# Who issues the last two transfers of score maxima in a fused two-layer cross-attention kernel

## The reference, cut to what matters

```python
q = hidden_state @ Wq + bq
k = encoder_hidden_state @ Wk + bk
v = encoder_hidden_state @ Wv + bv
scores = jnp.einsum('bkgld,bksd->bkgls', q, k) * scale + mask
attn = jax.nn.softmax(scores, axis=-1)
out = jnp.einsum('bkgls,bksd->bkgld', attn, v)
# ... output projection, residual, layer norm
```

## Time and profile before

| what | value |
|---|---|
| median of 3 runs | 886.73 us (885.75 to 888.23) |
| the profiled execution | 885.36 us, span 883.5 us |
| PE busy | 786.0 us, 89% |
| DVE busy | 597.9 us, 68% |
| ACT busy | 488.3 us, 55% |
| POOL busy | 561.7 us, 64% |
| mean granted TensorE clock | 0.943 of full speed |
| issues of qstack<-mrep | 64 by SPq, 128 KB each |

### The profile page before, as it was taken

The page is one execution under the profiler, slowest core; times in us unless marked ns, Lnnn a source line. Parts: engine busy times, 40 slices in busy tenths (PEclk is TensorE's granted clock), DMA queues, the critical chain, the costliest instruction groups (busy, mean ns, idle before and its releaser), DMA issues.

```text
span 883.5 us, 17327 instructions
## 1 busy us (share of the span) xinstructions
PE 786.0 (89%) x5015; PEld 619.9 (70%) x5015; DVE 597.9 (68%) x1016; ACT 488.3 (55%) x1067; POOL 561.7 (64%) x769
## 2 busy tenths in 40 slices
PE   6699989899898989989898999989899998988662
PEld 5576868678586867868686786868778686866431
DVE  4785948768485785858577685858768585866633
ACT  5547474655737465573746557374655747465050
POOL 3937494865858577585857658494866749473144
PEclk9989999999999999999999999999999999999776
DMA  8233252514334251433525143352514325242420
GB/s 315 65 102 96 73 132 90 144 56 112 101 101 119 86 144 66 110 104 101 125 86 150 58 115 96 100 131 89 142 62 118 99 89 131 89 96 72 101 84 24
DMA packets 58764, 92.23 MB, mean 104 GB/s; under 512 B 10480, under 2 KB 28528, under 8 KB 58608
## 3 DMA queue, kind: packets, MB, share of 16 engines
q1 hardware_dynamic: 58016, 91.60, 36.8%
q10 hardware_dynamic: 720, 0.28, 0.2%
HBM read 24.72 MB, written 8.39 MB: 37 GB/s over the span
## 4 chain that ended last, share of the span: by engine, by line
PE 62%; SPq 13%; DVE 8%; DMA 6%; issue 5%; POOL 5%; ACT 1%; DVEq 0%; POOLq 0%; ACTq 0%
PE banks L781 13%; SPq L373 12%; PE banks L872 11%; PE banks L885 7%; DMA qstack<-mrep 4%; PE banks L897 4%; DVE maxima L1527 4%; PE banks L899 4%; PE banks L898 4%; PE banks L819 3%; POOL atl L618 3%; PE banks L821 3%; PE banks L820 3%; PE banks L843 2%; DVE ql L1520 2%
## 5 line engine op out<-in xcount | busy, mean ns | idle before, releaser
L1477 DVE TENSOR_REDUCE negmax<-banks 128x1 f32<-128x512 f32 x128 | 84.5, 682 | 139.1 <-PE banks L768 139.1
L1527 DVE TENSOR_REDUCE maxima<-banks 128x4 f32<-128x512 f32 x256 | 160.1, 683 | 12.6 <-PE banks L843 12.5
L1184 ACT ACTIVATE prob<-banks 128x512 f32<-128x512 f32 x256 | 133.8, 607 | 33.8 <-PE banks L872 32.5
L872 PE MATMUL banks<-qstack,kstack 128*128 128x512 f32 x256 | 101.4, 527 | 39.4 <-DMA qstack<-mrep 38.9
L781 PEld LDWEIGHTS banks<-ta,att 128*128 128x128 f32 x1024 | 119.0, 190 | 4.1 <-POOL ta L553 1.3
L781 PE MATMUL banks<-ta,att 128*128 128x130 f32 x1024 | 119.6, 275 | 0.9 <-POOL ta L553 0.9
L872 PEld LDWEIGHTS banks<-qstack,kstack 128*128 128x128 f32 x256 | 61.1, 247 | 84.3 <-issue 74.2
L1553 DVE RECIPROCAL dens<-dens 128x512 f32<-128x512 f32 x32 | 107.1, 3346 | 17.3 <-DMA dens<-sides 17.3
L1118 ACT ACTIVATE att<-banks,negmax 128x512 f32<-128x512 f32 x128 | 87.4, 685 | 47.4 <-DVE negmax L1477 47.4
L618 POOL TENSOR_TENSOR atl<-at,ath 128x512 fp32r<-128x512 f32 x32 | 47.0, 1468 | 99.5 <-ACT ath L1196 99.5
L1169 ACT ACTIVATE qh<-banks,bq_s 128x256 fp32r<-128x256 f32 x64 | 30.4, 476 | 92.2 <-PE banks L821 92.2
(11 more groups left out here) (144 smaller groups left out, 1950.4 us busy)
## 6 DMA issues: line engine op xcount, KB each, us to landing
qstack<-qh SPq DMA_DIRECT2D x128, 128.0 KB, 2.3
xs<-in_x SPq DMA_DIRECT2D x16, 512.0 KB, 3.7
ys<-in_ctx SPq DMA_DIRECT2D x16, 512.0 KB, 3.7
kstack<-kph SPq DMA_DIRECT2D x128, 64.0 KB, 2.0
qstack<-ql SPq DMA_DIRECT2D x64, 128.0 KB, 2.3
qstack<-mrep SPq DMA_DIRECT2D x64, 128.0 KB, 2.3
dens<-sides SPq DMA_DIRECT2D x64, 128.0 KB, 2.0
out_x<-late SPq DMA_DIRECT2D x32, 256.0 KB, 2.1
```

What stands on the lines that cost most here:

```text
L872: last = mm(o, kstack[:, j, 2 * p + odd], qstack[:, p, j], start=True, stop=not masked)
L1184: nc.scalar.activation(prob[:, 2 * p + odd], banks[:, slot(plan, f"st{j}{kv}")], exp_f).then_inc(sem["prob_done"], 1)
L1527: nc.vector.tensor_reduce(maxima[:, 0, p, :, 2 * g:2 * g + 2], banks[:, slot(plan, f"mx{g}{p}")].rearrange("x (j o s) -> x j o s", j=2, o= ...
```

## The change

SyncE's `stack_maxima` issues the transfers of p = 0 and 1 only. Those of p = 2 and 3 are issued by ScalarE, in a new function `stack_last_maxima`, called ahead of the first exponential of the scores in both `iteration` and `last_iteration`. Shapes, tiles and semaphores of the transfers stay. ScalarE now waits for `mrep_done` there.

```diff
             def stack_maxima(q):
                 wait(sp, "mrep_done", q, 0)
-                for p in range(KV // 2):
+                for p in range(KV // 4):
                     sp.dma_start(qstack[96:96 + MROWS, p].bitcast(F32),
...
+            def stack_last_maxima(q):
+
+                wait(act, "mrep_done", q, 0)
+                for p in range(KV // 4, KV // 2):
+                    act.dma_start(qstack[96:96 + MROWS, p].bitcast(F32),
+                                 mrep[MROWS * p:MROWS * (p + 1)].bitcast(F32).unsqueeze(1).broadcast_to([MROWS, 2, G, P])
+                                 ).then_inc(maxrow_in[p], 16)
...
                     exp_energy(i, plan, 1, 1)
                 if s2:
+                    stack_last_maxima(q)
                     exp_scores(q, plan, 0, 0)
...
                     q_high(q, plan, 3)
+                    stack_last_maxima(q)
                     exp_scores(q, plan, 0, 0)
```

## The result

The changed kernel takes 930.00 us at the median (928.98 to 934.26), against 887.48 us of the kernel before in the same runs. The ratio is 1.0489, with a 95% interval of 1.0449 to 1.0529. The forecast was 901, with a range of 886 to 909: the sign was right and the size three times too small, 42.5 us instead of 14.

The account below looks back on a forecast made before the run. Landings of the third and fourth maxima were taken to pace TensorE's score products three and four. 6.3 + 8.3 - 0.5 + 0.1 = 14.2 us on 885.36, plus 1.37, gave 900.9, forecast 901.0 us; range 886.0 to 909.0.

Parts of the forecast that it names:

- (c): ScalarE's two transfers meet the ys load on the DMA engines: 0.7 us later, bounds 0 and 1.4.
- (d): Scores 0.9 us late at TensorE: half comes back as its clock rises, 0.45 us in 14 passes, 6.3 us.
- (e): TensorE's clock: the long slow stretch of pass 3 comes in 5 more passes, 1.65 us each, 8.3 us.
- (a): SyncE's queue: two issues fewer, ys load issued 1.28 us earlier, which hastens nothing that counts.
- (b): ScalarE's queue: third issue 0.2 to 1.1 us late, taken as 0.2; its two issues hidden before the score exponential.
- Rival 2: ScalarE's queue waits for its engine to end: issues late, scores 1.1 to 1.6 us late, 910; chance 0.12.
- (f): Pass 16, without ys: two queues issuing at once gain 0.5 us; pass 15 loses 0.1.
- rivals, 1: Delay swallowed: products three and four only 0.2 to 0.4 us late, no long slow stretch, 886 to 888.5; chance 0.26.
- Rival 3: Scores late as forecast, but TensorE's clock stays as before: +5.9 us, 892.6; chance 0.11.
- rival 4: Faster: first two maxima land earlier, idle too short for TensorE's clock to fall in two passes, 883.4; chance 0.06.

Follow-up runs that it names:

- short hold: Kernel before, all on SyncE's queue, with SyncE's third transfer of maxima held until the first has landed, ys behind all four: 920.33 us, ratio 1.0371.
- ys behind: Changed kernel, but ScalarE also issues the load of ys, behind its third and fourth transfer of maxima: 899.66 us, ratio 1.0119.
- ys in the middle: Kernel before, all on SyncE's queue, with the ys load issued between the second and third transfer of maxima: 932.38 us, ratio 1.0491.
- eighth of the load: Changed kernel with the ys load cut to 64 of 512 columns for both examples: 909.21 us, ratio 1.0252.
- all, on-chip: Changed kernel with the ys load for later pairs replaced by the same 512 KB from on-chip tile wq_h: 926.21 us, ratio 1.0456.
- long hold: Kernel before, with SyncE's third transfer of maxima held until the second has landed, ys behind all four: 933.34 us, ratio 1.0517.
- ys by ScalarE: Kernel before, all four maxima by SyncE, with the ys load issued by ScalarE behind its second energy exponential: 930.70 us, ratio 1.0472.
- the early issues: Against the kernel with ys behind on ScalarE's queue: ScalarE's two maxima issues moved ahead of both energy exponentials; 914.49 us, ratio 1.0313.
- both edits: Kernel with the queries' new order, plus ScalarE's maxima issues ahead of its energy exponentials and ys behind them: 897.14 us, ratio 1.0113.
- the queries' new order: Kernel before, with SyncE's eight query transfers of high parts issued first, the four of low parts behind: 883.47 us, ratio 0.9959.

## Why the prediction was wrong

Three terms failed. The meeting with ys (c) was sized at 0.7 us and measured 2.5. The price of a late score was too low in both of its parts: "half comes back" (d), and the long slow stretch in 5 more passes (e), where it came in 13 more. The short hold tells them apart: with scores only 1.0 us late, close to my 0.9, passes 1 to 14 cost 29.8 us, where (d) and (e) together had 14.6. The other 1.7 us of lateness take this to 44.3. So about half of the miss is (c), and half is the price.

**(a) SyncE, right in time, wrong in judgement.** Ys was issued 396.60 - 395.13 = 1.47 us behind the first maxima, 1.27 earlier than before; I had 1.28. I wrote that it hastens nothing that counts. It is some 31 of the 42 us, by the run with ys behind.

**(b) ScalarE's issues, right.** I took 0.2 us late; they were 0.1 late and hid behind the exponential, since the queue runs ahead of the engine. Rival 2, an issue that waits for the engine, is out: 396.58 lies ahead of the activation's start at 396.65. The Trainium skill's rule on the shared generator of descriptors ("Perfetto Trace Analysis", "DMA Instruction — HWDGE (DVE, Sync)") also gave a later third issue; it started within 0.02 us of that of ys and took 0.59 us, and that of ys took 0.46 as before, so nothing of a lock is seen there. In pass 16, where both queues issue at 883.03, a part of the rule may be seen: SyncE's two took 1.52 us instead of 1.29, and the first landed 0.8 us later.

**(c) The meeting with ys, too small.** I bounded it at 0 to 1.4 us and took 0.7. It was 2.5 (landing 4.8 instead of 2.3), beyond the upper bound of this term. (The 2.5 that I gave as the outer bound of the whole lateness is met by luck: it had 1.1 of a late issue in it, of which 0.1 came.) The bound was the time of the bytes. It holds for on-chip bytes, 1.4 us, but the load comes from off-chip: its own landing takes 4.2 us here, and the third transfer lands 0.6 us after it. The profile of before held the landing of ys in pass 7, and I used it for nothing:

```profile
DMA to landing us min/median/max: 3.4/3.4/3.4
```

Had I taken it as the earliest landing of what meets ys, the third transfer would have landed at 379.20 + 3.4 = 382.6, 1.3 us late, where I had 0.9. That is still half of what came: ys itself landed 0.8 us later than before, and the third transfer 0.6 us behind it, and no row of the kernel before shows either. The rule of the Trainium skill that I cited ("DMA: Bandwidth & Descriptors", "Issuing engines are not separate DMA queues") is borne out in that the queue does not matter: one queue with ys in the middle and two queues cost the same, 1.0491 and 1.0489. That transfers interleave gives no price: here they hardly did, and the small one ended behind the large one.

**(d) Half of the lateness comes back: not borne out.** In the table, the start of the third score is a median of passes 4 to 14 of the profiled execution, and the last two columns are of its passes 1 to 14.

| kernel | third score, us behind the first | passes with the long slow stretch | us in all |
|---|---|---|---|
| before | 1.21 | 1 | 719.9 |
| ys behind, on ScalarE's queue | 1.26 | 5 | 730.3 |
| eighth of the load | 1.81 | 7 | 739.5 |
| short hold | 2.17 | 10 | 749.7 |
| all, on-chip | 2.79 | 12 | 757.5 |
| long hold | 2.83 | 14 | 762.5 |
| changed | 3.92 | 14 | 764.2 |

I had priced a long stretch at 1.65 us at most, half of 3.3. (The lengths of pass 3 and pass 8 leave only 1.1 for it.) With 1.65 for each, what is left is at least 0.7, 1.1 and 1.5 us per pass for the eighth, the short and the long hold, which are 0.6, 1.0 and 1.6 us late: about the lateness in full and not half of it. For the changed kernel it is 1.6 us of 2.7. Why nothing comes back up to 1.6 us, and no more is lost beyond, was not shown.

**(e) The clock, right in kind, too small in number.** The mechanism of pass 3 is what happened, with 54.6 us in a pass instead of 51.2. I took the long stretch in 5 more passes, for 8 us; it came in all 14, 13 more, 21 us. That is at most half of the loss; the rest is the lateness itself. My prices with the measured lateness and count, 14 x 1.3 + 13 x 1.65 = 39.7, give 886.7 + 39.7 = 926, against 930. That this comes near is luck: for the short hold they give 14 x 0.5 + 9 x 1.65 = 21.9 in place of 29.8, and for the long one 32.7 in place of 42.6. By the table even the 0.9 us that I forecast would have brought the long stretch in 6 to 9 more passes.

**(f) Pass 16, no gain.** I expected 0.5 us of gain from two issuers at once. The first score came 0.8 us later, because the first landing takes longer when both queues start together and the third transfer goes in front. From its first transfer to the end the pass went from 54.3 to 55.05 us, which is no more than it varies between kernels that leave pass 16 as it was: 54.14 with ys in the middle, 56.12 with ys by ScalarE.

Of the rivals, 1 fell with (c). Its small price is doubtful as well: the kernel whose scores are only 0.05 to 0.15 us late is 11 us slower, though that it is they that cost it was not shown. Rival 3 fell with the clock, rival 4 had nothing for it.

## What to carry to other kernels

A small transfer that an engine is waiting for must not be issued behind a large load, or at the same moment, on whichever queue: take the landing time of that load as the least it will need, not the time of its bytes. Before an issue is taken off a queue, look at what the queue issues next, and whether that had been well placed behind the others by accident. Where TensorE's clock falls in each pass, less than a microsecond at that place decides between a short and a long slow stretch. Price a wait there by a run with a known hold: one pass of the trace that had a long stretch gave its kind here, but neither how often it comes nor what the lateness itself costs.

## What the runs showed of the hardware

- ScalarE's queue issues a transfer before the activation ahead of it in the program has started: 396.58, against 396.65.
- Transfers issued behind a 512 KB off-chip load, or 0.02 us ahead of it on the other queue, land after it, the first of them by 0.2 to 0.6 us, whether on its queue or on the other: 4.8 us from issue (two queues), 4.0 us from an issue 0.5 us behind that of the load (one queue). A transfer issued 0.3 us ahead of the load lands after 2.4. Next to the same load out of on-chip memory they land after 3.8.
- Of two queues that start within 0.4 us of each other, one has its first transfer landed after 2.5 to 3.2 us and the other after 3.2 to 3.5, against 2.4 for one queue alone, with no large load about. In pass 16 of the changed kernel and with the early issues it was the needed one that came second; with both edits together it was so in half of the passes.
- The passes settle at certain lengths, about 51.2 us in the kernel before and in the one with the queries' new order, 54.6 us in the changed kernel and in that with the long hold, and stay there over differences of 0.8 us and more in what is done. Why these lengths hold was not shown.
